# One pipeline through six stages: the tail of a stage carries the head of the next

## What is computed

```python
h = relu(layernorm(x))
# L0, two inner layers (gnn): scores h W h^T with a left and a right W, exp, times adj, normalised
#     h = relu(layer_norm(attention @ (h @ W_lin.T + b_lin), ln_a, ln_b))
# L1 (att1): 12 heads, softmax(q k^T / sqrt(32) + beta * adj, masked where adj is 0) @ v
# L2, two inner layers (digcn): a = softmax(h h^T / sqrt(384)) * adj, normalised
#     ctx = (a * upper) @ (h Wl) + diag(a) * (h Ws) + (a * lower) @ (h Wr); h = relu(layer_norm(ctx))
# L3 (att3): 12 heads, softmax(q k^T * scale + adj) @ v, then @ Wo.T + bo
x = x + layer(h)
```

## Time and profile before

| | |
|---|---|
| median of three runs | 3102.17 us (3102.14 to 3104.78) |
| profiled execution, own time | 3103.01 us |
| its span in the profile | 3101.1 us |
| mean granted TensorE clock | 0.967 |
| TensorE busy | 2798.5 us, 90% of the span |
| VectorE busy | 1955.9 us, 63% |
| ScalarE, GpSimd busy | 1032.2 us, 944.8 us |
| DRAM traffic | 68 GB/s over the span |

### The profile page before, as it was taken

The page is one execution under the profiler, slowest core; times in us unless marked ns, Lnnn a source line. Parts: engine busy times, 40 slices in busy tenths (PEclk is TensorE's granted clock), DMA queues, the critical chain, the costliest instruction groups (busy, mean ns, idle before and its releaser), DMA issues.

```text
span 3101.1 us, 71547 instructions
## 1 busy us (share of the span) xinstructions
PE 2798.5 (90%) x26048; PEld 2348.3 (76%) x26048; DVE 1955.9 (63%) x4550; ACT 1032.2 (33%) x1985; POOL 944.8 (30%) x874
## 2 busy tenths in 40 slices
PE   6999979999949999997999997999995799999998
PEld 5888868888847777776888886888884677777776
DVE  4445534555556676676777775677776577777775
ACT  3333423333324444443233322222221343333342
POOL 1211214444423333332011110244334244333433
PEclk9999989999979999998999998999998899999999
DMA  3222242333321112113122113222323011111110
GB/s 100 71 71 71 61 133 79 101 101 101 99 62 46 46 46 61 53 46 98 45 66 66 48 52 123 66 83 96 96 96 96 8 46 46 46 38 42 36 36 34
DMA packets 197215, 210.21 MB, mean 68 GB/s; under 512 B 72736, under 2 KB 197024, under 8 KB 197024
## 3 DMA queue, kind: packets, MB, share of 16 engines
q1 hardware_dynamic: 197024, 207.33, 21.8%
HBM read 131.80 MB, written 75.50 MB: 67 GB/s over the span
## 4 chain that ended last, share of the span: by engine, by line
PE 46%; DVE 15%; issue 8%; ACT 1%; POOL 1%; DMA 1%; DVEq 1%; POOLq 0%; ACTq 0%
PE psum L1016 15%; PE psum L825 14%; PE psum L829 4%; DVE v_x L1451 2%; DVE room L1709 2%; PE psum L854 2%; PE psum L1043 2%; PE psum L843 2%; PE psum L898 2%; DVE room L1479 2%; DVE room L1409 2%; PE psum L875 1%; DVE room L1495 1%; PE psum L866 1%; DMA w_raw<-w_all 1%
## 5 line engine op out<-in xcount | busy, mean ns | idle before, releaser
L1016 PE MATMUL psum<-fast 128*128 128x384 f32 x3456 | 656.5, 342 | 30.9 <-DVE room L1409 13.7
L1016 PEld LDWEIGHTS psum<-fast 128*128 128x128 f32 x3456 | 594.2, 188 | 83.6 <-DVE room L1409 38.4
L1409 DVE TENSOR_TENSOR room<-psum,rows 128x384 f32<-128x384 f32 x512 | 283.6, 555 | 298.5 <-PE psum L1016 159.6
L825 PE MATMUL psum<-fast 128*128 128x512 f32 x1728 | 460.4, 413 | 3.8 <-DVE fast L1439 3.0
L692 PE MATMUL psum<-fast 128*128 128x512 f32 x1728 | 411.6, 395 | 16.1 <-DVE fast L1396 16.1
L692 PEld LDWEIGHTS psum<-fast 128*128 128x128 f32 x1728 | 324.0, 189 | 100.8 <-issue 34.8
L825 PEld LDWEIGHTS psum<-fast 128*128 128x128 f32 x1728 | 321.5, 194 | 74.8 <-issue 4.9
L542 POOL TENSOR_TENSOR room<-room 128x768 f32<-128x768 f32 x128 | 188.5, 1473 | 477.6 <-DVE room L1485 295.9
L829 PE MATMUL psum<-fast 128*128 128x384 f32 x1152 | 235.5, 348 | 42.4 <-DVE v_x L1451 30.0
L1234 ACT ACTIVATE room<-psum 128x512 f32<-128x512 f32 x192 | 114.5, 596 | 398.6 <-PE psum L692 398.6
L829 PEld LDWEIGHTS psum<-fast 128*128 128x128 f32 x1152 | 195.1, 188 | 63.3 <-DVE v_x L1451 41.4
(11 more groups left out here) (108 smaller groups left out, 4319.2 us busy)
## 6 DMA issues: line engine op xcount, KB each, us to landing
x_ring<-x_mid SPq DMA_DIRECT2D x64, 768.0 KB, 4.7
x_mid<-x_ring SPq DMA_DIRECT2D x48, 768.0 KB, 4.1
x_ring<-x_in SPq DMA_DIRECT2D x32, 768.0 KB, 4.7
z_mid<-x_ring SPq DMA_DIRECT2D x32, 768.0 KB, 4.1
z_sb<-z_mid SPq DMA_DIRECT2D x32, 768.0 KB, 6.0
out<-x_ring SPq DMA_DIRECT2D x16, 768.0 KB, 4.0
w_raw<-w_all SPq DMA_DIRECT2D x19, 576.0 KB, 4.4
adjc<-adj SPq DMA_DIRECT2D x64, 128.0 KB, 3.8
```

What stands on the lines that cost most here:

```text
L825: mm = nc.tensor.matmul(dst, wpart[m][:, c, oc * P:(oc + 1) * P], hpart[G.par][:, c], start=(k == 0), stop=(k == 3 * C - 1))
L1016: mm = nc.tensor.matmul(dst[:, 0:H], hpart[G.par][:, c, first_row:first_row + P], wpart[m][:, c, :], start=(k == 0), stop=(k == 3 * C - 1))
L1409: done(nc.vector.tensor_tensor(dst, src, rows[:, m], ALU.add), "evac_n")
```

## The change

Bodies get three groups (g, F, X) that know their stage: they mix g, project F and normalise X. In the last two bodies of a stage, F and X may be of the next stage ("lead"). The last body of stage 1 and of stage 4 is a new function `to_att`, that of stage 2 `to_gcn`, on each of the four compute engines; the separate beginnings of the stages 1 to 5 and `enter` are gone.

The weights have six slots in place of four, three for even and three for odd stages (att3's fourth goes into slot 0); the raw buffer is double; the loads for the next stage are issued from body 12 on, and VectorE splits the first two in body 14 and the others in body 15. To make room, the projected tiles of gnn (`lin`) and gcn (`lin3`) have one set of buffers in place of two, and the gcn affine works in place (`y4c` is `c4`). So an eviction into these buffers waits for the mix of the group before (`cx`), or, for the middle matrix, for its gather (`cc`). At the start, v_x is cleared at the kernel's beginning and not ahead of att1, and the second group of x is loaded behind the second weight matrix.

The diff, cut to its core (the two functions `to_att` are of VectorE and of GpSimd):

```diff
-        w_raw = sb("w_raw", [P, C, H])
-        fast = sb("fast", [P, 8 * C * H + 4 * C * (GT + S) + 4 * H], F32R)
-        rows = sb("rows", [P, 5, H])
+        w_raw = sb("w_raw", [P, 2, C, H])
+        fast = sb("fast", [P, 12 * C * H + 4 * C * (GT + S) + 4 * H], F32R)
+        rows_all = sb("rows", [P, 8, H])
...
-        w_hi = [f32r(m * WM, C, H) for m in range(4)]
-        w_lo = [f32r((4 + m) * WM, C, H) for m in range(4)]
...
+        w_hi = [f32r(m * WM, C, H) for m in range(6)]
+        w_lo = [f32r((6 + m) * WM, C, H) for m in range(6)]
...
-        ROOM = 17280
+        ROOM = 12352
...
-        lin = take(2, T, H + 1)
...
+        lin = take(T, H + 1)
...
-        lin3 = take(2, 3, T, H)
+        lin_l = take(T, H)
+        lin_s = take(T, H)
+        c4 = take(T, H)
+        y4c = c4
...
+        lin_r = take(T, H)
...
-        def sweep(eng, body):
...
+        def sweep(eng, n, body, cross=None):
 
             with eng.Fori(0, LOOP) as turn:
                 for p in (0, 1):
-                    body(Group(turn, p), True, True)
-            body(Group(LOOP, 0), True, False)
-            body(Group(LOOP, 1), False, False)
+                    g = Group(n, turn, p)
+                    body(g, g + 1, g + 2)
+            g, h = Group(n, LOOP, 0), Group(n, LOOP, 1)
+            if n + 1 == len(PHASES):
+                body(g, h, None)
+                body(h, None, None)
+            else:
+                lead = Group(n + 1, 0, 0, lead=True)
+                body(g, h, lead)
+                (cross or body)(h, lead, lead + 1)
+
+        def rows(G):
+            return rows_all[:, 0:5] if G.n % 2 == 0 else rows_all[:, 5:8]
+
+        def w_slot(G, m):
+            return (0, 1, 2)[m] if G.n % 2 == 0 else (3, 4, 5, 0)[m]
+
...
+            def load_w(n, m):
+                k = w_total(n - 1) + m
+                if k >= 2:
+                    sp.wait_ge(w_split, 2 * (k - 1))
+                sp.dma_start(w_raw[:, k % 2], w_view[PHASES[n]["mats"][m]]).then_inc(w_in[k % 2], 16)
+
+            def load_rows(n):
+                for i, r in enumerate(PHASES[n]["rows"]):
+                    sp.dma_start(rows(Group(n, 0, 0))[:, i], v_all[r:r + 1, :].to_broadcast([P, H])).then_inc(par_in, 16)
...
+                    if more and k == 0:
+                        load_rows(n + 1)
                         load_w(n + 1, 0)
-                        if nxt["norm"]:
-                            load_z(g + 2, 0)
-                    if nxt and k == 3:
-                        for m in range(1, len(nxt["mats"])):
-                            load_w(n + 1, m)
-                    body(g, k < 3, k < 2)
...
-                def next_w(g, t, one):
-
-                    if one or n + 1 == len(PHASES):
-                        return
-                    if t == 0:
-                        after(dve, "pp", g, st["pp"].per - 1)
-                    for m in range(len(PHASES[n + 1]["mats"])):
-                        if min(m, T - 1) == t:
-                            split_w(n + 1, m)
...
+            def next_w(F, X, *ms):
+
+                if X and X.lead:
+                    split_w(X.n, *[m for m in ms if m < 2])
+                elif F and F.lead:
+                    split_w(F.n, *[m for m in ms if m >= 2 and m < len(PHASES[F.n]["mats"])])
...
+            def c_nat(G, i):
+
+                if G.lead and i == 0:
+                    dve.wait_ge(par_in, par_total(G.n))
+                m, t = divmod(i, T)
+                after(dve, "pp", G, i)
+                if m == 1:
+                    after(dve, "cc", G + -1, T - 1)
+                else:
+                    after(dve, "cx", G + -1, 1)
+                done(nc.vector.tensor_tensor(lin3[m][:, t], bank_of(G, G_SLOT[i])[:, 0:H], rows(G)[:, m], ALU.add),
+                     "evac_n")
...
+            def to_att(g, F, X):
+
+                stats_of(X, 0)
+                if g.kind == "gnn":
+                    n_context(g)
+                    stats_of(X, 1)
+                    n_scale(g)
+                else:
+                    for k in range(T):
+                        c_gather(g, k)
+                    c_variance(g)
+                    stats_of(X, 1)
+                    c_scale(g)
+                shift_of(X)
+                split_w(F.n, 2)
+                add_x(g, 0, 1, 2, 3)
+                a_bias(F)
+                if F.third:
+                    split_w(F.n, 3)
+                split_h(F, X, 0)
+                a_nat(F, 0)
+                split_h(F, X, 1)
+                a_soft(F, 0)
+                a_nat(F, 1)
+                split_h(F, X, 2)
+                a_nat(F, 2)
+                a_soft(F, 1)
+                a_sums(F, 0)
+                a_nat(F, 3)
+
+            def to_gcn(g, F, X):
+
+                def nat(*js):
+                    for j in js:
+                        c_nat(F, j)
...
+            def to_att(g, F, X):
+
+                (n_sigma if g.kind == "gnn" else c_sigma)(g)
+                norm_root(X)
+                for t in range(T):
+                    affine(g, t)
+                a_shift(F, 0)
+                a_shift(F, 1)
+                a_weigh(F, 0)
...
+                sweep(dve, n, *((n_body,), (n_body, to_att), (a_body, to_gcn), (c_body,), (c_body, to_att), (a_body,))[n])
```

2623 lines of the change are left out of this document (1270 added, 1353 removed), and 2 rows, old and new, of the table used.

## The result

The changed kernel takes 3030.89 us (median of four runs, 3028.66 to 3031.5) against 3102.64 us of the kernel before, run beside it. The ratio is 0.9766, with a 95% interval of 0.9749 to 0.9783: faster by 2.3%. The forecast was 3019.

What follows compares the result with a forecast made beforehand. Crossings were taken as bound by a serial chain, mid-stage by TensorE with VectorE's evictions close behind. 3103.0 - 163 (surplus) + 47 (kept by crossings) + 32 (gcn) + 1 (start) = 3020, as median 3019 us; range 2955 to 3070.

Steps and rivals of the forecast that it cites:

- The surplus of the crossings: Five stage crossings: time beyond two bodies' work, summed to 163 us, the most the change can win.
- gcn's 32 us: 28 gcn loop bodies: part 0's eviction waits for the mix's last quarter, chain 1.13 us later each, 32 us lost.
- The two chains into att: Last bodies of stages 4 and 1: affine, adds, split, evictions of v; mix to next body 43 and 29.5 us.
- Body 14 of stages 4 and 1: Last-but-one bodies of the stages before att: 4 us lost in stage 4, 5 in stage 1.
- 0 to 1: Crossing from stage 0 to 1: only splits and normalisations between evictions, 2 us kept of the 22.3 surplus.
- The start: Kernel's beginning: second x load stands behind a weight load, charged 1 us.
- The rule on the common port pair: VectorE and GpSimd lock shared ports per instruction; seven splits into att, if all charged, cost 8 us more.
- The hidden wait: Rival in the gcn bodies: the new eviction wait costs nothing, 2987 us; chance 0.20.
- the dearer crossings: Rival at the crossings: they keep twice as much, 94 us, kernel 3066 us; chance 0.15.
- the free ones: Rival: crossings keep only some 15 us and gcn loses nothing, 2955 us; chance 0.07.
- The clock: Rival in 28 gcn bodies: more waiting lowers TensorE's granted clock, 49 us, kernel 3068 us; chance 0.08.
- the slower case: Rival at the crossings: carried groups do not overlap, all 163 us given back, 3136 us; chance 0.05.

Runs made afterwards that it cites:

- the split's run: Changed kernel with the split of att3's fourth weight at the end of stage 4's last body, not ahead of the first eviction of v: 3022.2 us.
- the new order: Changed kernel with last bodies into att reordered: first eviction of v ahead of adds, fourth split last, ScalarE's evictions ahead of scaling, GpSimd weighing tile 0 earlier: 3024.7 us.
- the run with two buffers: Changed kernel, but the first tile of the left projection in the gcn stages has two buffers again, for even and odd groups: 3001.6 us.

## Why the prediction was right, and where its sizes were off

- **The surplus of the crossings, 163 us.** It could be checked only with what was kept: the crossings gave 108.7 of it, forecast 116. Three crossings came within 1.6 us of the forecast; the bound of two bodies' work was a good one in stage 3, where with the splits moved the tail bodies took 28.29 and 28.12 us. Of the signs, the granted clock and the periods came as forecast, and one came better: TensorE's longest wait behind the start is 4.27 us, where waits of 10 us or more were allowed ahead of att3. No run keeps early weights without carried groups, so how much of the 108.7 is due to each is not shown.
- **gcn's 32 us.** Measured 32.2, and three runs show the step itself: mostly undone by one tile's buffer, nearly halved by one moved line, and in the first gcn stage turned into a gain by filling the wait. The two halves were not alike, +1.29 and +1.00 for 1.13 forecast, so the close sum has some luck in it; the delay of the chain was 1.02 in the body shown.
- **The two chains into att.** From the mix to att3's body 43 was forecast and 43.0 measured, for att1 29.5 and 29.4. For att3 the pieces fit as well: 24.2 us from the mix to the first eviction of v and 18.8 from there, for 23.6 and 19.3 forecast. For att1 the sum is luck: the last mix of stage 1 begins at 853.32 (821.40 + 31.92), and with the row below the pieces are 18.9 and 10.5 us, where 16.9 and 12.6 were forecast. The affine, the adds and the split were the chain, as the 1.84 us of the split's run and the 8 of the new order show. What I had not walked is the chain beside it, normalisation to transposed tile, which took the place of the first when that was shortened.

```profile
872.23 1.45 DVE L1502 TENSOR_TENSOR v_x<-psum,rows 64x192 f32<-64x192 f32 x4
```

- **Body 14 of stages 4 and 1: mis-sized.** I took 4 and 5 us; 8.7 (36.49 against 27.78) and 6.5 (31.92 against 25.42) were measured; other runs of the same bodies differ by up to 2 us. In stage 1 one split gave back 4.0, a part of which is the lower clock behind its wait; in stage 4 three waits of TensorE add up to 6.2, of which the first, 2.92, stands behind the split and two are for transposed tiles, which I had left out.
- **0 to 1: too small, and wrong in kind.** I charged 2 us to splits; 4.1 were lost (55.0 against 50.9), and moving two of the splits gave none of it back: 2.14 us of waiting for nothing that the profile shows and a part at lower speed behind it (3.51 for 2.25) are 3.4 of it. This is the gap in a carried body that I had named as a sign of being wrong.
- **The start: failed.** I charged 1 us to the order of the loads, and said nothing of the clearing that the change moves. Measured were 3.9, and the clearing is their cause, by a longer wait and the lower clock behind it: with the clearing first, the first mix is between 1.4 us earlier and 0.8 us later than in the kernel before.
- **The rule on the common port pair.** I cited it against the splits; of the seven splits into att three were slowed, each in one of its halves and by 0.7 to 0.8 us (1.55 for 0.76, 2.04 and 2.05 for 1.36), about 2 us in place of the 8. It decided at the start, where a single GpSimd instruction of 2.73 us held a VectorE cast 2.68 us longer than in the kernel before. The Trainium skill, "SBUF — State Buffer", section "🔬 SBUF: two separate sides", has the loser blocked for the whole instruction, and this row agrees.
- **The rivals.** The hidden wait falls with the gcn periods, the dearer crossings (94) and the free ones (15) with the 54.3 us that the crossings kept. The clock falls in the loop, with the window of the body shown above (the second row here, in windows' columns: busy time of PE, PEld, DVE, ACT and POOL, PEclk, DMA share, GB/s): waits of 0.59, 0.39 and 0.90 us leave it at 1.00. In the crossings and at the start it did cost time, which I had not counted there: the first row is the crossing from stage 0 with its wait of 2.14 us, and the start's 0.79 and the 0.71 ahead of att3 stand above.

```profile
435.00:445.00 10.00, 8.97 (x41) 6.04 (x42) 4.29 (x16) 1.20 (x2) 1.01 (x1) 0.83 0.01 2
1600.00:1625.00 25.00, 22.70 (x192) 19.20 (x185) 17.25 (x46) 7.89 (x19) 3.45 (x4) 1.00 0.22 68
```

Nothing pointed to the slower case.

## What to carry to other kernels

Where a stage's end is a serial chain, measure the distance between the same mark in the last full body and in the next stage's first, and take the work of the bodies between from it: that is all an overlap can win. Walk the new order on each queue for what is kept, and every moved instruction on every engine, a clearing at the start too. When a buffer is halved to pay for it, look for the one tile whose eviction now waits: a single tile's buffer gave back most of the loss here, one line moved nearly half of it. And where a tail body makes TensorE wait, look at the granted clock behind the wait before the whole price is put down to the instruction that caused it.

## What the runs showed of the hardware

- A clearing on GpSimd (128 x 3168, 2.73 us) held a VectorE cast, which takes 0.42 us alone, for 2.68 us more than the 0.96 that it takes beside the GpSimd instruction ahead of the clearing. Which of the two comes first differs between runs: in seven of eight profiles the clearing did; in the one where the cast did, it took 0.96 us, as it does with the clearing elsewhere.
- TensorE waited 2.11 to 2.14 us at the same place, at the end of body 14 of stage 0, in all eleven profiles of the changed kernel and its variants, for nothing that the profile shows. I have no experiment on its cause.
- What this wait of some 2 us costs behind it varies from run to run, and the granted clock goes with it: the nine matmuls behind it took 3.51 us in the changed kernel, with the clock of the 10 us from 435 on at 0.83, and 2.32 in the run with two buffers, with the clock there at 1.00, against 2.25 in a body before. Of the eleven profiles, four have 2.32 to 2.33 us for them and seven 3.03 to 3.89. By the marks the crossing from stage 0 lies between 53.5 and 55.1 us in runs whose code is the same there.
